# A decoder layer's cross-attention in steps of two head groups, with the feed-forward products of the second sequence's head phase spread in quarters and 32 turns ahead of the first load

## The chip, the cores and the metric

The kernel runs on one core of one Trainium2 chip. The metric is the device time of one execution in microseconds (us); "before" is the median of three runs. Engines are named as in the profile: PE is TensorE (PEld its weight loads, SPq, POOLq and so on an engine's issuing side), DVE is VectorE, ACT is ScalarE, POOL is GpSimd, SP is SyncE, which issues all DMAs.

## The reference, cut to what matters

Two sequences of 1024 tokens with 256 features pass through one post-norm decoder layer: causal self-attention with rotary embedding (16 heads of 16), cross-attention to 77 context tokens, and a feed-forward part of five matrices. Each is followed by a residual addition and a layer norm.

```
x = _layernorm(x + _L0_attn_ref(x, w_qkv, w_proj))
x = _layernorm(x + _L0_xattn_ref(x, ctx_1024, ctx_1024, mask, Wq, bq, Wk, bk, Wv, bv, Wo, bo))
    # q, k, v in 16 heads of 16; scores (1024 x 77 a head), mask, softmax over 77, times v, times Wo
x = _layernorm(x + _L0_ffn_ref(x, w1, w2, h1, h2, w3))
    # silu(x w1) * (x w2), gelu(. h1), gelu(. h2), . w3
```

## The kernel before, in words

Every engine runs its own written-out program, and semaphores are the only ties. There is no scheduler: the order on an engine is the order in which the code issues. `wait(eng, q, name, n)` waits for a counter of sequence q. The stages of a sequence follow one another, and where the first sequence's feed-forward is due, its products are dealt out over the second sequence's stages by a table (`PLAN`, `F_MM`): a slot is one step of a stage, and `f_products(slot, ...)` issues the products of that slot. `f_work` does the other engines' part of a finished group one slot later.

- **Start.** `projections` makes q, k and v token block by token block (8 blocks of 128 tokens): `project_qk` (L557), `project_v` (L566) and, at block 1, `project_ctx` (L575, L578) on TensorE, `rope` (L1097 to L1099) on VectorE, `rope_add` on GpSimd. VectorE and GpSimd first wait for all small weights (`w_in`, nine loads), TensorE for `set_dve` 4 (VectorE's mask work).
- **Self-attention, "S".** Steps -20 to 49. The steps below 0 are the head phase: `turn` (L599) transposes the staged heads, `max_unit` (L613) makes score blocks only to find row maxima, which `reduce_unit` (L1144, L1146) takes on VectorE. A step has up to four units, in pairs on the two halves of the array's rows (partitions 0 to 63 and 64 to 127). In the second sequence they have two PSUM banks, so unit n waits for the reduction of unit n-2. In that phase of the second sequence the first sequence's products (L834, L831, L822) all stand behind the step's units.
- **Cross-attention, "X".** A token block has 4 groups of 4 heads, and a step is one group: 32 steps a sequence. `x_unit` (L740 mask, L743 three products over 64 rows, 312 columns wide) makes the scores in one of two banks, `x_softmax` on VectorE takes the maximum (L1231) and subtracts it (L1235), `x_turn` (L753, four transposes) runs two steps later into one of two banks, `x_exp` (L1011) is ScalarE's, `x_values` (L764) comes four steps later. Once a block, `x_y_evac` (L1019), `x_y_turn` (L775) and `x_y_norm` (L1190, L1192) normalise its output, and the norm chain follows: transpose "yt" (L686, ScalarE L983), "proj" (L694), `residual` with its statistics on VectorE (L1216 or L1219, L1196, L1198), GpSimd's reciprocal root, `ln_finish` (L1203), transpose "xt" (L702, ScalarE L990), then `q_add` (L1224) or `input_lo` (L1241). "yt" and "xt" share bank 0, "proj" and "q" bank 1.

X(0) runs beside nothing but its own norms until its last steps, which take the first w1 and w2 products (slots from `FFN_STEP` to `X_END`). The second sequence's X is the same.

## Time and profile before

| | us |
|---|---|
| median of 3 runs (957.48 to 961.47) | 957.93 |
| the profiled execution's own time | 960.31 |
| its span, first to last instruction | 958.6 |
| TensorE busy | 881.7 (92%) |
| VectorE, ScalarE, GpSimd busy | 507.0, 377.2, 313.2 |

The profile is one execution. Busy time of TensorE is modelled from pipelined instructions that overlap, so 92% does not mean that it works at its peak; what one kind of work costs is read from the distance between the starts of successive instructions. The mean granted clock is 0.956 of full speed.

### The profile page before, as it was taken

To read this page: it belongs to the slowest core of one execution; us is meant where nothing else is said; L and a number is where in the kernel's file an instruction comes from. 1 tells how busy PE (TensorE), PEld (TensorE's weight loads), DVE (VectorE), ACT (ScalarE), POOL (GpSimd) and SP (SyncE) were. 2 spreads that over 40 slices of the span, in tenths; PEclk is the share of its full clock that TensorE was granted. 3 is DMA by queue.
4 is the path that set the end of the run, shared out by engine and by line. 5 is a ranking of instruction groups with operands and counts; after the bars stand their busy time and mean duration, and the time that the engine had idled before them with its cause. 6 is when DMAs were issued, how large, how long until landed. Compare 5 with 4: busy or idle time off the path is not lost.

```text
span 958.6 us, 14238 instructions
## 1 busy us (share of the span) xinstructions
PE 881.7 (92%) x5034; PEld 579.7 (60%) x5034; DVE 507.0 (53%) x1363; ACT 377.2 (39%) x790; POOL 313.2 (33%) x553
## 2 busy tenths in 40 slices
PE   5789999899999999988989899999999999999996
PEld 2544444346666777876666644443476667887885
DVE  4597888526565632165343678883366653116113
ACT  0566666673334311132111166666633343122210
POOL 4403224236101534344222223223440024335332
PEclk9956999989999999999989989998999999999999
DMA  9800533330000322323222033340000000000000
GB/s 310 333 1 3 186 124 133 123 130 1 1 2 1 104 95 92 128 100 121 88 88 88 13 122 133 134 155 2 1 2 1 1 1 1 1 1 23 1 1 24
DMA packets 23896, 68.71 MB, mean 72 GB/s; under 512 B 4400, under 2 KB 11568, under 8 KB 23600
## 3 DMA queue, kind: packets, MB, share of 16 engines
q1 hardware_dynamic: 23824, 67.77, 20.0%
q8 instruction: 43, 0.70, 0.3%
q14 instruction: 29, 0.24, 0.1%
HBM read 65.40 MB, written 13.63 MB: 82 GB/s over the span
## 4 chain that ended last, share of the span: by engine, by line
PE 76%; DVE 13%; issue 4%; ACT 3%; POOL 3%; SPq 1%; DMA 0%; POOLq 0%; DVEq 0%; ACTq 0%
PE bank L834 24%; PE bank L662 7%; PE bank L644 7%; PE bank L613 6%; PE bank L822 4%; PE bank L743 4%; DVE max_raw L1144 4%; PE bank L753 4%; DVE bank L1146 4%; PE bank L831 3%; PE bank L599 3%; PE bank L694 3%; PE bank L557 2%; PE bank L764 2%; PE bank L711 1%
## 5 line engine op out<-in xcount | busy, mean ns | idle before, releaser
L974 ACT ACTIVATE prob_s<-bank 128x512 f32<-128x512 f32 (+3 forms) x384 | 163.5, 497 | 80.3 <-PE bank L644 79.7
L1428 POOL TENSOR_TENSOR hid_lo_s<-act_raw_s,hid_hi_s 128x512 fp32r<-128x512 f32 x96 | 123.7, 1289 | 215.1 <-DVE hid_hi_s L1298 180.3
L613 PE MATMUL bank<-k_t_s,q_t_s 64*128 64x512 f32 (+3 forms) x384 | 141.1, 465 | 26.3 <-DVE max_raw L1146 15.3
L1298 DVE CAST hid_hi_s<-act_raw_s 128x512 fp32r<-128x512 f32 x64 | 30.5, 477 | 195.4 <-ACT act_raw_s L1035 195.1
L1146 DVE CUSTOM_DVE_ANT_0 bank<-bank,causal_bf 128x128 f32<-128x128 f32 (+3 forms) x256 | 122.8, 511 | 18.9 <-PE bank L613 16.8
L1399 POOL TENSOR_SCALAR_AFFINE_SELECT prob_s<-prob_s 128x128 f32<-128x128 f32 x256 | 72.0, 295 | 166.8 <-ACT prob_s L974 163.5
L644 PE MATMUL bank<-q_t_s,k_t_s 64*128 64x512 f32 (+3 forms) x384 | 115.2, 408 | 2.5 <-issue 1.6
L1035 ACT ACTIVATE act_raw_s<-bank,scales 128x512 f32<-128x512 f32 x64 | 43.7, 688 | 183.6 <-PE bank L834 183.6
L613 PEld LDWEIGHTS bank<-k_t_s,q_t_s 64*128 64x128 f32 x384 | 64.9, 205 | 70.2 <-DVE max_raw L1146 30.7
L644 PEld LDWEIGHTS bank<-q_t_s,k_t_s 64*128 64x128 f32 x384 | 58.5, 195 | 76.1 <-ACT prob_s L974 51.9
L1144 DVE TENSOR_REDUCE max_raw<-bank 128x1 f32<-128x512 f32 x128 | 82.4, 685 | 37.2 <-PE bank L613 37.2
L834 PE MATMUL bank<-hid_hi_s,home_s 128*128 128x512 f32 x256 | 99.9, 390 | 0.6 <-POOL hid_lo_s L1428 0.6
L834 PE MATMUL bank<-hid_lo_s,home_s 128*128 128x512 f32 x256 | 99.7, 390 | 0.0
L662 PE MATMUL bank<-prob_s,v_sb_s 128*32 128x512 f32 (+3 forms) x768 | 86.4, 523 | 3.3 <-POOL prob_s L1399 2.8
L834 PE MATMUL bank<-hid_hi_s,ring_s 128*128 128x512 f32 x192 | 78.3, 408 | 0.0
L834 PE MATMUL bank<-hid_lo_s,ring_s 128*128 128x512 f32 x192 | 76.9, 401 | 0.0
L1011 ACT ACTIVATE prob_s<-bank 77x512 f32<-77x512 f32 x64 | 37.9, 592 | 77.7 <-PE bank L753 77.7
L834 PEld LDWEIGHTS bank<-hid_hi_s,home_s 128*128 128x128 f32 x256 | 48.1, 188 | 11.3 <-issue 1.4
L834 PEld LDWEIGHTS bank<-hid_lo_s,home_s 128*128 128x128 f32 x256 | 48.1, 188 | 9.9
L1406 POOL TENSOR_SCALAR ln_var<-ln_mean 128x1 f32<-128x1 f32 x32 | 7.9, 248 | 135.6 <-DVE ln_mean L1198 135.6
L557 PE MATMUL bank<-w_qkv,x_t_s 128*128 128x512 f32 x64 | 32.1, 634 | 12.2 <-DMA w_qkv<-in_w_qkv 9.4
L753 PE MATMUL bank<-ident,xdiff_s 128*77 128x128 f32 x256 | 42.2, 288 | 0.2 <-issue 0.2
(154 smaller groups left out, 1516.1 us busy)
## 6 DMA issues: line engine op xcount, KB each, us to landing
ring_s<-scratch SPq DMA_DIRECT2D x34, 512.0 KB, 3.3
home_s<-scratch SPq DMA_DIRECT2D x22, 512.0 KB, 6.0
checked_s<-in_w_ffn SPq DMA_DIRECT2D x2, 3584.0 KB, 17.8
scratch<-in_w_ffn SPq DMA_DIRECT2D x2, 2560.0 KB, 10.6
ring_moved_s<-scratch SPq DMA_DIRECT2D x10, 512.0 KB, 3.1
checked_s<-in_w_ffn SPq DMA_DIRECT2D x1, 4096.0 KB, 32.2
x_t_s<-in_x_t SPq DMA_DIRECT2D x2, 1024.0 KB, 5.5
x_tok_s<-in_x SPq DMA_DIRECT2D x2, 1024.0 KB, 9.3
```

Of the source, the lines that this page charges most:

```text
L557: i = mm(bank[QK_BANKS[q][t % 2]][:], x_t[q][:, k, P * t:P * (t + 1)], L["w_qkv"][:, k, 0:2 * D], start=k == 0, stop=k == KD - 1)
L613: mm(out[:, 0:k1 - k0], qkt(q, p, 0)[r, P * qt:P * (qt + 1)], qkt(q, p, 1)[r, k0:k1], start=True, stop=True).then_inc(S["max_mm"], 1)
L644: mm(S_BANK[j][:, 0:CHUNK - q0], qkt(q, p, 1)[r, P * kb:P * (kb + 1)], qkt(q, p, 0)[r, CHUNK * c + q0:CHUNK * (c + 1)], start=True, stop=T ...
L662: m = mm(Y[32 * j:32 * (j + 1), q0:CHUNK], v_window(v_sb[q][:, kb], 4 * g + j), prob[q][4 * (s % 2) + j][:, 0:CHUNK - q0], start=kb == 0, ...
L753: m = pe.transpose(out[0:CTX, P * j:P * (j + 1)], xdiff[q][n % 4][:, j, 0:CTX], ident[:])
L834: o = mm(out[:], view(tile_h(f_weights(q, n, 0)[:], k), True), view(src[part][:, k]), start=i == 0, stop=i == last)
L974: act.activation(prob[q][4 * (s % 2) + j][:, 0:n], S_BANK[j][:, 0:n], ACT.Exp, scale=SCALE).then_inc(S["exp_done"], 1)
L1035: act.activation(act_raw[q][r % 3][:], f_bank(n)[:], ACT.Gelu, scale=scales[:, 1 + LAYER_NUMBER[layer], m:m + 1]).then_inc(S["f_act"], 1)
L1144: dve.tensor_reduce(dst, out[:], AXX, ALU.max).then_inc(S["max_red"], 1)
L1146: dve.tensor_tensor_reduce(out=out[:, 0:left], in0=out[:, 0:left], in1=L["causal_bf"][:, CHUNK - left:CHUNK], scale=1.0, scalar=NEG, op0=A ...
L1399: pool.affine_select(out=pr, in_=pr, compare_op=ALU.is_ge, fill=0.0, base=0, pattern=[[1, P]], channel_multiplier=-1).then_inc(S["select_d ...
L1428: pt(dst[1][:, m], act_raw[q][r % 3][:], dst[0][:, m].bitcast(F32), ALU.subtract).then_inc(S["f_lo"], 1)
```

## The change

Four edits. (1) Cross-attention takes two groups a step: 16 steps a sequence. The two groups' units lie in the two banks of one pair (tensor `bank_pair` of two banks), their products alternate between the two halves of the array's rows, and maximum, subtraction and exponential are one instruction each for both groups. There is one pair for units and one for turns, where there were two single banks for each. The turn comes one step later, the values two; on TensorE the values now stand ahead of the turn, and the turn ahead of the products of the slot. ScalarE's "yt" copy and output copy move ahead of the exponential. (2) VectorE's order in a step becomes softmax, finish, residual, output's normalisation; it was softmax, output's normalisation, residual, finish. (3) In self-attention steps a slot's products are issued in four quarters behind the four unit positions. Only the second sequence's head phase has such products. (4) At the start TensorE turns the identity 32 times as soon as GpSimd has written it, ahead of the wait for the first loads; the waits for the small weights move to their first users. The slots of X shrink from 11 to 6 a sequence, so each takes 10 or 11 of the 64 w1 and w2 products instead of 5 or 6.

```diff
+WARM = 32
-XN = NT * NG
-XTURN, XVALUES, XY = 2, 4, 2 * NG + 1
-X_NORM = XY + 2
+XG = NG // 2
+XN = NT * XG
+XTURN, XVALUES, XY = 1, 2, 2 * XG
+X_NORM = XY + 1
 FFN_STEP = XN + 1
-X_END = NG * (NT - 1) + X_NORM + 5
+X_END = XG * (NT - 1) + X_NORM + 4
-    lags = {"yt": (0, 0), "proj": (1, 1), "xt": (3, 4), "q": (4, None)}
+    lags = {"yt": (0, 0), "proj": (1, 1), "xt": (3, 3), "q": (4, None)}
-XUNIT_BANKS = (2, 3)
-XTURN_BANKS = (4, 5)
+XUNIT_PAIR, XTURN_PAIR = 1, 2
...
         def x_unit(q, n):
-            t, g = divmod(n, NG)
+            t, first = n // XG, 2 * (n % XG)
             if n == 0:
                 wait(pe, q, "ctx_blocks", 4)
                 wait(pe, q, "exp_done", 4 * LAST)
-            if g == 0:
+            else:
+                wait(pe, q, "xsub", n)
+            if first == 0:
                 wait(pe, q, "q_hi", t + 1)
                 wait(pe, q, "q_lo", t + 1)
-            if n >= 2:
-                wait(pe, q, "xsub", n - 1)
...
+            for i in range(2):
+                mm(x_units[:, i, 0:4 * CP].rearrange("p (j k) -> p j k", k=CP), L["ident_bf"][:], mask, start=True, stop=False)
+            for part, (of_q, of_k) in enumerate(((0, 0), (0, 1), (1, 0))):
+                for i in range(2):
+                    half, r = (first + i) // 2, slice(SLOT * i, SLOT * (i + 1))
+                    m = mm(x_units[:, i, 0:4 * CP], xq_hl[q][of_q][r, half, P * t:P * (t + 1)],
+                           kx_blocks[of_k][r, half].rearrange("p j k -> p (j k)"), start=False, stop=part == 2)
...
         def x_turn(q, n):
             wait(pe, q, "xsub", n + 1)
-            if n >= 2:
-                wait(pe, q, "xexp_done", n - 1)
+            if n:
+                wait(pe, q, "xexp_done", n)
...
-        def f_products(slot, exact):
+        def f_products(slot, exact, part=0, parts=1):
             if slot is None:
                 return
-            for q, n, i in F_MM[slot]:
+            work = F_MM[slot]
+            for q, n, i in work[len(work) * part // parts:len(work) * (part + 1) // parts]:
                 f_product(q, n, i, exact)
...
                     if kind == "y" and j == 3 and y_step(i) == s:
                         y_turn(q, i)
-            f_products(slot, exact)
+                f_products(slot, exact, j, 4)
...
             if s < XN:
                 x_unit(q, s)
-            if 0 <= s - XTURN < XN:
-                x_turn(q, s - XTURN)
             norm_products(q, "X", s, ("yt", "proj"))
-            f_products(slot, exact)
             if 0 <= s - XVALUES < XN:
                 x_values(q, s - XVALUES)
-            if s >= XY and (s - XY) % NG == 0 and (s - XY) // NG < NT:
-                x_y_turn(q, (s - XY) // NG)
+            if 0 <= s - XTURN < XN:
+                x_turn(q, s - XTURN)
+            if s >= XY and (s - XY) % XG == 0 and (s - XY) // XG < NT:
+                x_y_turn(q, (s - XY) // XG)
+            f_products(slot, exact)
             norm_products(q, "X", s, ("xt", "q"))
...
         pe.wait_ge(set_pool, 11)
-        pe.wait_ge(set_dve, 4)
+        for i in range(WARM):
+            m = pe.transpose(R[:, P * (i % 4):P * (i % 4 + 1)], ident[:], ident[:])
+        m.then_inc(S["warm_mm"], 1)
         wait(pe, 0, "x_t_in", 16)
         pe.wait_ge(L["w_qkv_in"], 16)
         for t in range(NT + V_LAG):
             projections(0, t)
+        pe.wait_ge(set_dve, 4)
...
         def cross_attention(q, s):
             if s < XN:
                 x_softmax(q, s)
-            if s >= XY and (s - XY) % NG == 0 and (s - XY) // NG < NT:
-                x_y_norm(q, (s - XY) // NG)
-            norm_work(q, "X", s)
+            norm_finish(q, "X", s)
+            norm_work(q, "X", s, ("proj",))
+            if s >= XY and (s - XY) % XG == 0 and (s - XY) // XG < NT:
+                x_y_norm(q, (s - XY) // XG)
+            norm_work(q, "X", s, ("rest",))
...
         dve.wait_ge(L["rope_in"], 16 * 2)
-        dve.wait_ge(w_in, 16 * 9)
```

**TensorE in the middle of X(0).** Before, these rows are two groups of a token block, that is two steps. Bank numbers stand behind `bank`, and `xdiff` is the difference that the turn reads, `prob` what the values read.

```order
L740 MATMUL bank3<-xmask_bias,ident_bf 128x312
L743 MATMUL bank3<-kx_blocks_hi,xq_hi_s0_137 128x312
L743 MATMUL bank3<-kx_blocks_lo,xq_hi_s0_137 128x312
L743 MATMUL bank3<-kx_blocks_hi,xq_lo_s0_138 128x312
L753 MATMUL bank5<-ident,xdiff1_s0_142 77x128 x4
L686 MATMUL bank0<-ident,tok0 128x128 x2
L764 MATMUL bank6<-prob3_s0_88,vx 32x128 x4
L702 MATMUL bank0<-ident,tok0 128x128 x2
L740 MATMUL bank2<-xmask_bias,ident_bf 128x312
```

In the changed kernel the same place, one step with both groups, reads so on TensorE:

```order
L745 MATMUL bank_pair1<-xmask_bias,ident_bf 128x312 x2
L749 MATMUL bank_pair1<-kx_blocks_hi,xq_hi_s0_137 128x312 x2
L749 MATMUL bank_pair1<-kx_blocks_lo,xq_hi_s0_137 128x312 x2
L749 MATMUL bank_pair1<-kx_blocks_hi,xq_lo_s0_138 128x312 x2
L691 MATMUL bank_pair0<-ident,tok0 128x128 x2
L772 MATMUL bank_pair3<-xprob3_s0_150,vx 32x128 x8
L760 MATMUL bank_pair2<-ident,xdiff2_s0_143 77x128 x8
L745 MATMUL bank_pair1<-xmask_bias,ident_bf 128x312 x2
```

The masks, the three products, the turns and the values of two groups now stand together, and the values come ahead of the turn. Before, "xt" (L702) followed "yt" (L686) in the same step; now it is gone from this step and stands in the other step of the block, as L707.

**TensorE in the head phase of the second sequence.** Before, one whole step's units and turn (L613, L599) between two slots' products (L834); `k_t0`, `q_t0` are the turned heads of the first pair.

```order
L834 MATMUL bank5<-hid0_lo_s0_161,ring1_s1_177 128x512
L613 MATMUL bank0<-k_t0_s1_74,q_t0_s1_73 128x512
L613 MATMUL bank1<-k_t0_s1_74,q_t0_s1_73 128x512
L599 MATMUL bank6<-ident,stage_q_s1_61 128x128 x4
L613 MATMUL bank0<-k_t0_s1_74,q_t0_s1_73 128x256
L613 MATMUL bank1<-k_t0_s1_74,q_t0_s1_73 128x256
```

After it, two of a step's four units (L618), with the quarter of five products (L842) between them and the turn (L604) behind the second:

```order
L618 MATMUL bank_pair0<-k_t0_s1_74,q_t0_s1_73 128x512
L842 MATMUL bank_pair2<-hid0_lo_s0_167,ring0_s1_182 128x512
L842 MATMUL bank_pair2<-hid0_hi_s0_166,ring0_s1_182 128x512
L842 MATMUL bank_pair2<-hid0_lo_s0_167,ring0_s1_182 128x512
L842 MATMUL bank_pair2<-hid0_hi_s0_166,ring0_s1_182 128x512
L842 MATMUL bank_pair2<-hid0_lo_s0_167,ring0_s1_182 128x512
L618 MATMUL bank_pair0<-k_t0_s1_74,q_t0_s1_73 128x512
L604 MATMUL bank_pair3<-ident,stage_q_s1_61 128x128 x4
L842 MATMUL bank_pair2<-hid0_hi_s0_166,ring1_s1_183 128x512
```

The two units of a pair no longer stand together; each is an island between products.

**VectorE in X(0).** Before, the end of one step with its residual (L1216), and the next step, which ends with the output's normalisation (L1190, L1192):

```order
L1235 TENSOR_TENSOR xdiff0_s0_141<-bank2,xmax 128x4x77
L1216 SCALAR_TENSOR_TENSOR resid0_s0_131<-bank1,no_key,x_tok_s0_57 128x256
L1196 BN_STATS ln_stats<-resid0_s0_131 128x6
L1198 BN_AGGR ln_mean<-ln_stats 128x2
L1231 TENSOR_REDUCE xmax<-bank3 128x4
L1235 TENSOR_TENSOR xdiff1_s0_142<-bank3,xmax 128x4x77
L1190 RECIPROCAL recip<-bank7 128x16
L1192 TENSOR_TENSOR tok0<-bank7,recip 128x256
```

In the changed kernel, one early step with two groups' softmax, finish, residual and normalisation:

```order
L1250 TENSOR_REDUCE xmax<-bank_pair1 128x8
L1254 TENSOR_TENSOR xdiff1_s0_142<-bank_pair1,xmax 128x8x77
L1222 TENSOR_SCALAR tok0<-resid0_s0_131,ln_mean,ln_rstd 128x256
L1238 TENSOR_TENSOR resid1_s0_132<-bank_pair0,x_tok_s0_57 128x256
L1215 BN_STATS ln_stats<-resid1_s0_132 128x6
L1217 BN_AGGR ln_mean<-ln_stats 128x2
L1209 RECIPROCAL recip<-bank_pair3 128x16
L1211 TENSOR_TENSOR tok0<-bank_pair3,recip 128x256
```

The softmax is half as many instructions of twice the width, and residual and normalisation fall into the same step.

## Rows read from the trace of the kernel before

**Rows 1.** The page's chain that ended last, shares of the span by engine.
```profile
PE 76%; DVE 13%; issue 4%; ACT 3%; POOL 3%; SPq 1%; DMA 0%; POOLq 0%; DVEq 0%; ACTq 0%
```

**Rows 2.** Busy us (instructions) by stretch: X(0) to its last softmax, second head phase.
```profile
core 0: us, PE busy (x) PEld busy (x) DVE busy (x) ACT busy (x) POOL busy (x), PEclk, DMA share, GB/s
225.00:303.00 78.00, 75.47 (x612) 50.63 (x611) 50.43 (x122) 28.99 (x60) 16.49 (x31) 1.00 0.01 1
445.00:552.00 107.00, 94.20 (x403) 67.92 (x402) 48.54 (x140) 17.91 (x29) 27.91 (x28) 0.94 0.20 72
```

**Rows 3.** TensorE's waits in 225 to 303 us: total, times, longest.
```profile
PE bank L702 <- ACT y_t_s L983: 2.3, 5, 0.5
```

**Rows 4.** Timeline of TensorE, one group's step of X(0) and the output's turn.
```profile
start us, us, engine line op out<-in xcount [idle before <-releaser]
295.67 0.31 PE L740 MATMUL bank<-xmask_bias,ident_bf 128*128 128x312 bf16 x1
295.91 0.41 PE L743 MATMUL bank<-kx_blocks_hi,xq_hi_s 64*128 64x312 f32 x1
296.16 0.30 PE L743 MATMUL bank<-kx_blocks_lo,xq_hi_s 64*128 64x312 f32 x1
296.30 0.30 PE L743 MATMUL bank<-kx_blocks_hi,xq_lo_s 64*128 64x312 f32 x1
296.53 0.66 PE L753 MATMUL bank<-ident,xdiff_s 128*77 128x128 f32 x4
297.12 0.43 PE L764 MATMUL bank<-prob_s,vx 77*32 77x128 f32 x8
297.48 0.66 PE L775 MATMUL bank<-ident,y_sb_s 128*128 128x128 f32 x4
297.97 0.30 PE L740 MATMUL bank<-xmask_bias,ident_bf 128*128 128x312 bf16 x1
```

**Rows 5.** Timeline of VectorE and ScalarE, durations at two widths each.
```profile
222.50 0.69 DVE L1166 COPY y_sb_s<-bank 128x512 f32<-128x512 f32 x1 [1.41 <-PE bank L662]
...
292.25 0.37 ACT L983 ACTIVATE y_t_s<-bank 128x256 f32<-128x256 f32 x1
...
297.15 0.48 DVE L1235 TENSOR_TENSOR xdiff_s<-bank,xmax 128x308 f32<-128x308 f32 x1
297.23 0.59 ACT L1011 ACTIVATE prob_s<-bank 77x512 f32<-77x512 f32 x1 [2.08 <-PE bank L753]
```

**Rows 6.** TensorE's waits in 445 to 556 us.
```profile
PE bank L613 <- DVE max_raw L1146: 7.4, 5, 1.8
PE bank L613 <- DVE max_raw L1144: 4.6, 16, 0.8
```

**Rows 7.** Timeline of TensorE in one step of the second head phase.
```profile
510.33 0.39 PE L834 MATMUL bank<-hid_hi_s,ring_s 128*128 128x512 f32 x1
510.56 0.39 PE L834 MATMUL bank<-hid_lo_s,ring_s 128*128 128x512 f32 x1
510.87 0.50 PE L613 MATMUL bank<-k_t_s,q_t_s 64*128 64x512 f32 x2
511.30 0.66 PE L599 MATMUL bank<-ident,stage_q_s 128*128 128x128 f32 x4
...
513.69 0.50 PE L834 MATMUL bank<-hid_hi_s,ring_moved_s 128*128 128x512 f32 x1
514.03 0.39 PE L834 MATMUL bank<-hid_lo_s,ring_moved_s 128*128 128x512 f32 x1
```

**Rows 8.** Timeline of the start, and turns at half clock (last row).
```profile
3.78 0.53 POOL L1483 TENSOR_SCALAR_AFFINE_SELECT causal_bf<-causal_bf 128x128 bf16<-128x128 bf16 x1
9.43 5.78 PE L557 MATMUL bank<-w_qkv,x_t_s 128*128 128x512 f32 x8 [9.43 <-DMA w_qkv<-in_w_qkv]
16.17 0.69 DVE L1097 TENSOR_TENSOR rope_a_s<-bank,cos_t 128x512 f32<-128x512 f32 x1 [9.88 <-DMA blocks<-in_blocks]
29.34 1.88 PE L557 MATMUL bank<-w_qkv,x_t_s 128*128 128x512 f32 x4
37.56 1.06 PE L599 MATMUL bank<-ident,stage_q_s 128*128 128x128 f32 x8 [1.16 <-DVE stage_k_s L1132]
61.00 1.09 PE L599 MATMUL bank<-ident,stage_q_s 128*128 128x128 f32 x4 [1.13 <-issue]
```

97 lines of the change are left out of this document (54 added, 43 removed).

## The prediction

> **What bounds the kernel.** I read the chain that ended last first: TensorE holds 76% of it [rows 1]. An edit pays where it makes TensorE's own sequence shorter or takes a wait out of it. The busy time by stretch comes next. In cross-attention up to its last softmax (225 to 303 us, 32 steps) TensorE is busy for 75.5 of 78 us, at full clock, and the other engines for far less [rows 2]; its waits there are 2.3 us, five of about 0.5 us, all "xt" behind ScalarE's "yt" copy out of the bank that both use [rows 3]. So a step takes 78 / 32 = 2.4 us and is TensorE's own work. In the second head phase (445 to 552 us) TensorE is idle for 12.8 of 107 us and its granted clock is 0.94 [rows 2]. Of two levels, 0.94 means 12% of the time at the half one, about 12.8 us in which half the speed is lost: 6.4 us of full-speed work. Its waits there are 12.0 us, all for VectorE's reductions [rows 6].
>
> **Cross-attention: what a pair of groups costs.** "Busy" hides what matters, so I take starts from the timeline of one step [rows 4]. The mask starts at 295.67, the products at 295.91, 296.16 and 296.30, the turns at 296.53: 0.86 us for a unit, of which 0.24, 0.25, 0.14 and 0.23 lie between those starts. 312 columns at 2.4 GHz are 0.13 us, so only the third gap is near its work; the others have 0.1 us on top, where the array goes from one shape of work to another (128 rows, 64 rows, 128 rows) or where the next weights go to the same half. The turns take 0.59 us for four (to 297.12) and the values 0.36 us (to 297.48); the turns themselves run 0.11 us apart, as the output's four show (0.49 us to 297.97).
>
> In the changed step both units stand together, their products alternate between the halves, and each change of shape is paid once for two groups. What two products on different halves cost is in the head phase: two 512-column units in one row end after 0.50 us, and the next work starts 0.43 us after them [rows 7]; two in turn would be 0.21 us longer. So they run beside each other. The pair: masks 0.13 + 0.24, products 0.25 + 0.14 + 0.23, together 0.99 us, against 2 x 0.86 = 1.72: 0.73 saved. Eight turns in a row: 0.59 + 4 x 0.11 = 1.03 against 1.18: 0.15 saved. Sixteen value products: the 0.36 us hold two passes of 0.13, so 0.36 + 0.27 = 0.63 against 0.72: 0.09 saved. That is 0.97 us a pair, **15.5 us a sequence** for 16 pairs. The bound on the other side: if the halves took turns, three products of 0.13 us would come back, 0.39 us a pair or 6.2 us a sequence.
>
> **What it adds there.** With one pair of banks a unit waits for the softmax of the step before. Width costs VectorE (0.69 - 0.48) / 204 = 1.03 ns a column [rows 5], so 616 columns take 0.48 + 0.32 = 0.80 us, twice that for maximum and subtraction. With the last product's 0.30 us [rows 4] and about 0.15 us for three hand-overs the next unit can start 2.05 us after the last product starts. TensorE meanwhile has at least 0.23 + "yt" 0.2 + values 0.63 + turns 1.03 = 2.1 us in the lean step of a block and over 3 us in the other. That is covered, but barely. Not covered is step 1 of each sequence, with only "yt" between the first two units: **1.5 us**. The exponential of 1024 columns takes 0.59 + 2 x 0.22 = 1.0 us [rows 5] and must end ahead of the next values; behind it on ScalarE stands the copy "xt" (0.37 us), then `input_lo`, then "yt" on the same bank. From the end of the turns: 0.2 + 1.0 + 0.4 + 0.5 = 2.1 to 2.2 us, against y turn 0.49 + "xt" 0.25 + unit 0.99 = 1.73 us on TensorE: a new wait of 0.45 us a block for about six blocks, **2.7 us**. At the end, where no unit follows, values and turns wait twice for the exponential, **1.0 us**. The five waits of rows 3 go (2.3 us), since "xt" now stands in the other step. The 64 w1 and w2 products and the rest of the tail are the same work in fewer steps; I count them at nothing. ScalarE's and VectorE's part of them is covered by 10 or 11 products of 0.23 us a slot (2.4 us) against 1.55 us for a pair's activation and gate, and if that cover fails it costs some tenths a slot.
>
> VectorE's new order costs nothing: in a block's fuller step it has 1.6 softmax, 1.1 residual and statistics, 0.7 normalisation and 0.4 `input_lo`, less than TensorE's 4.3 us, and the residual's input is there earlier than the normalisation's.
>
> Sum for a sequence: 15.5 + 2.3 - 1.5 - 2.7 - 1.0 = 12.6 us. Both: **-25.2 us**. Ends: -12.7 (halves take turns) and -32.6 (no new wait but the first).
>
> **Head phase in quarters.** Of 12.0 us of waits [rows 6] nearly all can go: a quarter is 5 products of 0.23 us (510.33 to 510.56 [rows 7]), 1.2 us, longer than a 0.69 us reduction and its hand-over. And with no idle stretches the clock should not fall, which is worth 6.4 us. Against it stand the islands. Going from products into a unit takes 0.31 us instead of 0.23; a unit's way out 0.43 instead of 0.21; and the first product behind it 0.34 instead of 0.23 (513.69 to 514.03) [rows 7]: 0.08 + 0.22 + 0.11 = 0.41 us an island. Before, a step has about 1.0 us of this (one way in and out, and the way to and from the turn); afterwards four islands, 1.7 us. A pair that ran side by side now runs apart, 0.2 us more. That is +0.9 us a step, 13 us in 14 steps. Sum -12.0 - 6.4 + 13 = **-5 us**. Ends: -12 if the islands cost half of that, +3 if the clock falls all the same.
>
> **Start.** Before, the first product starts at 9.43 us, and eight take 5.78 us [rows 8], at full clock 8 x 0.43 = 3.4 (four take 1.88 with their last one's tail). 5.6 us to the eighth's end without its tail are five products at 0.85 and three at 0.43, so the clock rose some 4.3 us after the first one started. The identity is ready at 4.3 us (the last row of GpSimd before it ends at 3.78 + 0.53). A turn is 1.06 / 8 = 0.11 to 0.13 us at full clock, and about 0.22 at the half (four in 1.09) [rows 8]. If turns raise the clock as those products did, it rises at about 8.7 us, after 20 turns; 12 more end at 9.9 to 10.1. The eight products then end at 13.3 instead of 15.0. VectorE's first rotation, which waited until 16.17 for the last small weight, can start at 11.8. TensorE goes on with what lies before the last q/k product at 29.34 [rows 8]: 8.6 us of q/k and 1.7 of v products, and 4.0 us that hold the context's products and waits for VectorE; of these I take 0.6 away, since VectorE's context sums still stand between its rotations. That gives 27.1, **-2.2 us**, which reaches the first turn at 37.56 through rotation, sum and staging unchanged.
>
> The Trainium skill, "TensorE: Matmul & The Clock Gate", Part 4, speaks against this: it says that transposes do not count as TensorE's work for the clock in the way products do. No row here settles that, for no stretch is turns alone. By that rule this term would be the +1.3 us of the third rival below.
>
> **Sum.** -25.2 - 5 - 2.2 = -32.4 us. Against the profiled execution's own 960.31 us that is 927.9. The median of the runs is 2.4 us lower, 957.93, so the time is **925.5 us**.
>
> **Rivals.**
> *Half a gain in cross-attention.* The halves take turns where both accumulate, or VectorE's chain of maximum and subtraction takes 0.4 us longer than its width says and shows in every lean step. X then gives 12 to 16 us, and the time is 935 to 945 us. For it: the margin of the lean step is nil. Against: two units in 0.50 us.
> *The islands eat the head phase.* As many changes of shape again and a clock that still falls: +3 instead of -5, 933 us.
> *Turns do not raise the clock.* 32 turns at half clock end at 4.4 + 7.0 = 11.3 us, the products start 1.9 us late and again at half clock. VectorE's early rotations give back some 0.6 us of this: +1.3 us instead of -2.2, 929 us. I give it 0.4, inside the forecast's own range.
> *No change.* TensorE's sequence gets shorter, but the waits behind it grow as much: 955 to 960 us.
> *Slower.* VectorE is a queue: if in both steps of a block its softmax stands behind `input_lo`, which waits for ScalarE behind the exponential, a step becomes TensorE's whole step plus copy, `input_lo` and the part of the softmax that the unit doesn't cover: 3.6 + 0.4 + 0.4 + 0.9 = 5.3 us against 4.8 for two steps now, +16 us, 974 us. It decides once the new wait is over (25.2 + 5 + 2.2) / 32 = 1.0 us in every step beyond those counted. Only one of a block's two steps has `input_lo`, so I give it little.
>
> **How the numbers follow.** The forecast (X at -20 to -33, head phase at -10 to +1, start at -4 to +1) has 0.62 and 914 to 935 us. Half a gain in X 0.20; the head phase at +3 with a full X 0.05; more than 44 us gained 0.03; no change 0.06; slower 0.04. The range 914 to 941 us takes in the forecast and most of the second and third case. A difference of 0.5% (4.8 us) is about what this measurement can tell from none. Faster by more: 0.62 + 0.20 + 0.05 + 0.03 = 0.90; same 0.06; slower 0.04.
>
> **What would show it.** In the profile after: a pair of units with 0.99 us from mask to the next work and the two products of a pair starting together (1.4 us would be the halves in turns); a token block in 7.2 to 7.7 us instead of 9.6; TensorE's longest wait in X for the subtraction in step 1, 1.5 us, and small ones of "yt" for `input_lo`; maximum and subtraction at 0.80 us each. In the head phase no wait for a reduction over 1 us, a granted clock of 1.00, and 5 us less. At the start, whether the eight q/k products run 0.43 us or 0.85 us apart. The prediction is wrong if TensorE waits in each lean step for the subtraction, or if the islands cost more than 0.41 us.

## The result and the profile after

The changed kernel takes 928.22 us (median of 4 runs, 927.68 to 932.09), beside 959.26 us of the kernel before on the same chip; the ratio is 0.968, with a 95% interval of 0.965 to 0.971. A second set of 6 runs gave 925.39 us and 0.965 (0.961 to 0.970), so the gain is 31 to 33 us. The prediction was 925.5 us, in a range of 914 to 941.

On the page of the changed kernel, the engines' busy time and the chain that ended last, by engine:

```profile
PE 865.7 (93%) x5066; PEld 572.7 (62%) x5066; DVE 499.5 (54%) x1299; ACT 374.1 (40%) x758; POOL 313.4 (34%) x553
PE 78%; DVE 13%; ACT 3%; issue 3%; POOL 2%; POOLq 0%; DVEq 0%; ACTq 0%
```

TensorE held 76% of the chain [rows 1]; it holds 78% of a shorter one. The change shortened TensorE's own sequence and the bound is still there.

I cut each trace into stages at the first instruction of a kind (first staged turn, first unit's score, first mask, first w1 or w2 product, and so on). The table gives each stage's length in us, with the time at half granted clock in parentheses. The zeros of the first row mean little: the trace holds no clock record for its first 9 to 14 us, in which TensorE ran at half speed. "Again" is the changed kernel's second profile; "best" is the last kernel of this study.

```
stage                          before       after        again        best
start, to the first turn       37.6 ( 0)    35.0 ( 0)    35.2 ( 0)    35.1 ( 0)
first head phase               40.8 (34)    40.7 (29)    40.8 (33)    40.7 (29)
self-attention 0              147.1 (17)   146.2 (15)   146.2 (15)   146.0 (15)
cross-attention 0              80.5 ( 0)    67.3 ( 0)    67.4 ( 0)    64.7 ( 0)
w1 and w2 slots behind it      22.0 ( 0)    20.4 ( 0)    20.3 ( 0)    20.3 ( 0)
q/k/v products 1               94.0 ( 3)    95.0 ( 3)    95.0 ( 3)    95.2 ( 7)
second head phase             129.2 (14)   122.3 ( 0)   122.3 ( 0)   106.1 ( 0)
self-attention 1              146.2 (14)   153.9 (41)   146.3 (14)   146.0 (14)
cross-attention 1              80.3 ( 0)    67.2 ( 0)    67.2 ( 0)    64.7 ( 0)
w1 and w2 slots behind it      20.7 ( 0)    19.2 ( 0)    19.2 ( 0)    19.2 ( 0)
feed-forward to the end       160.2 ( 3)   163.1 ( 7)   161.5 ( 4)   161.5 ( 3)
```

The change's three places give 2.4 us (start), 14.7 us a sequence (cross-attention and the slots behind it) and 6.9 us (head phase). The two cross-attention rows have to be read together. In the kernel before, the values of three groups (1.1 us) and one turn of the output (0.4 us) lie behind the first w1 or w2 product; in the changed kernel they lie ahead of it. So 1.5 of the 1.6 us that the second row lost only moved to the first. The one stage of before against after that goes the other way is self-attention 1, where no instruction changed: in that execution its clock was at the half level for 41 us. In "again" it wasn't, and the span was 921.4 us instead of 930.3.

*Cross-attention.* Busy time by stretch in the profile after, to be held against rows 2 (the first line is the block of X(0), the second the head phase):

```profile
219.00:285.00 66.00, 62.60 (x640) 47.12 (x642) 47.33 (x97) 28.39 (x47) 17.29 (x32) 1.00 0.01 1
420.00:530.00 110.00, 108.06 (x435) 69.48 (x434) 55.44 (x156) 22.12 (x35) 32.23 (x35) 0.99 0.23 75
```

The timeline of TensorE in one token block of the first cross-attention, after:

```profile
257.61 0.43 PE L745 MATMUL bank_pair<-xmask_bias,ident_bf 128*128 128x312 bf16 x2
...
259.05 0.41 PE L691 MATMUL bank_pair<-ident,tok 128*128 128x128 f32 x2 [0.38 <-DVE x_lo_s L1260]
259.39 0.65 PE L772 MATMUL bank_pair<-xprob_s,vx 77*32 77x128 f32 x16
259.96 1.10 PE L760 MATMUL bank_pair<-ident,xdiff_s 128*77 128x128 f32 x8
260.90 0.44 PE L745 MATMUL bank_pair<-xmask_bias,ident_bf 128*128 128x312 bf16 x2
261.27 0.41 PE L749 MATMUL bank_pair<-kx_blocks_hi,xq_hi_s 64*128 64x312 f32 x2
261.52 0.30 PE L749 MATMUL bank_pair<-kx_blocks_lo,xq_hi_s 64*128 64x312 f32 x2
261.66 0.31 PE L749 MATMUL bank_pair<-kx_blocks_hi,xq_lo_s 64*128 64x312 f32 x2
261.89 1.13 PE L699 MATMUL bank_pair<-w_o,y_t_s 128*128 128x256 f32 x4
262.95 0.65 PE L772 MATMUL bank_pair<-xprob_s,vx 77*32 77x128 f32 x16
263.53 1.10 PE L760 MATMUL bank_pair<-ident,xdiff_s 128*77 128x128 f32 x8
264.46 0.60 PE L783 MATMUL bank_pair<-ident,y_sb_s 128*128 128x128 f32 x4
264.90 0.38 PE L707 MATMUL bank_pair<-ident,tok 128*128 128x128 f32 x2
265.12 0.44 PE L745 MATMUL bank_pair<-xmask_bias,ident_bf 128*128 128x312 bf16 x2
```

A pair of units takes 0.99 us (260.90 to 261.89), where two single ones took 1.72 [rows 4]: the gaps are 0.37, 0.25, 0.14 and 0.23, the ones that the prediction added up. The two products of one row cost the gap of one, so the halves work side by side. The values take 0.57, the turns 0.93. The block is 7.51 us (257.61 to 265.12), inside the 7.2 to 7.7 forecast.

TensorE's waits in this cross-attention, after (total, times, longest), and VectorE's two wide operations:

```profile
PE bank_pair L691 <- DVE x_lo_s L1260: 2.8, 5, 1.3
PE bank_pair L745 <- DVE xdiff_s L1254: 1.5, 1, 1.5
PE bank_pair L772 <- ACT xprob_s L1023: 0.2, 1, 0.2
...
250.74 0.80 DVE L1250 TENSOR_REDUCE xmax<-bank_pair 128x8 f32<-128x616 f32 x1 [0.47 <-PE bank_pair L749]
251.58 0.80 DVE L1254 TENSOR_TENSOR xdiff_s<-bank_pair,xmax 128x616 f32<-128x616 f32 x1
```

The forecast said 2.7 us for "yt" behind `input_lo`, 1.5 us in step 1, 0.80 us at 616 columns, and no wait in the lean steps. All four stand here. The end of the sequence waits 0.2 us and not 1.0.

*Head phase.* Its reductions held TensorE for 13.3 us before; rows 6 show 12.0 of them, because their window opens 23 us after the phase begins. None of these waits is left from 404 to 530 us after. The first two lines are before (421.9 to 551.2 us), the third is the longest that is left, after, on the first score behind the phase:

```profile
PE bank L613 <- DVE max_raw L1146: 8.7, 6, 1.8
PE bank L613 <- DVE max_raw L1144: 4.6, 16, 0.8
...
PE bank_pair L649 <- DVE resid_f_s L1285: 1.7, 1, 1.7
```

*Start.* TensorE from its first instruction on, after: the first 22 turns, the last 11 (the windows share one), the first eight products, and VectorE's first rotation; the last row is the busy time of 4.1 to 8.8 us, with the columns of rows 2:

```profile
4.13 4.95 PE L919 MATMUL bank_pair<-ident 128*128 128x128 f32 x22 [4.13 <-POOL causal_bf L1511]
8.66 1.51 PE L919 MATMUL bank_pair<-ident 128*128 128x128 f32 x11
10.01 3.60 PE L562 MATMUL bank_pair<-w_qkv,x_t_s 128*128 128x512 f32 x8
12.03 0.69 DVE L1116 TENSOR_TENSOR rope_a_s<-bank_pair,cos_t 128x512 f32<-128x512 f32 x1 [4.12 <-PE bank_pair L562]
...
4.10:8.80 4.70, 4.67 (x22) 4.67 (x23) 3.75 (x3) 0.00 (x0) 2.44 (x3) 1.00 1.04 389
```

From 4.13 to 8.66 us the turns start (8.66 - 4.13) / 21 = 0.22 us apart, from there to 10.01 1.35 / 11 = 0.12 us. The level went from the half to the full one near 8.7 us, with only turns on TensorE so far, and the eight products ran at 0.43 us each. The prediction had 8.7, 9.9 to 10.1, and 11.8 for the rotation.

### The profile page after: what moved, and what is told of

Same layout as the page of the kernel before. It is cut to its first block, busy times and chain, and to the rows that moved or that the text cites. A ratio compares the mean times of both kernels' runs of the same rounds, so it can differ in the third digit from the quotient of the medians.

```text
span 930.3 us, 14113 instructions
## 1 busy us (share of the span) xinstructions
PE 865.7 (93%) x5066; PEld 572.7 (62%) x5066; DVE 499.5 (54%) x1299; ACT 374.1 (40%) x758; POOL 313.4 (34%) x553
## 4 chain that ended last, share of the span: by engine, by line
PE 78%; DVE 13%; ACT 3%; issue 3%; POOL 2%; POOLq 0%; DVEq 0%; ACTq 0%
PE bank_pair L842 25%; PE bank_pair L667 7%; PE bank_pair L649 7%; PE bank_pair L618 7%; PE bank_pair L830 6%; DVE bank_pair L1165 4%; PE bank_pair L760 4%; DVE max_raw L1163 3%; PE bank_pair L699 3%; PE bank_pair L839 3%; PE bank_pair L604 3%; PE bank_pair L562 2%; PE bank_pair L772 2%; PE bank_pair L749 2%; PE bank_pair L716 1%
## 5 line engine op out<-in xcount | busy, mean ns | idle before, releaser
L986 ACT ACTIVATE prob_s<-bank_pair 128x512 f32<-128x512 f32 (+3 forms) x384 | 163.5, 495 | 86.7 <-PE bank_pair L649 85.8
L618 PE MATMUL bank_pair<-k_t_s,q_t_s 64*128 64x512 f32 (+3 forms) x384 | 149.2, 467 | 13.7 <-DVE max_raw L1165 7.6
L1165 DVE CUSTOM_DVE_ANT_0 bank_pair<-bank_pair,causal_bf 128x128 f32<-128x128 f32 (+3 forms) x256 | 123.4, 509 | 54.0 <-PE bank_pair L618 52.6
L649 PE MATMUL bank_pair<-q_t_s,k_t_s 64*128 64x512 f32 (+3 forms) x384 | 119.0, 423 | 3.9 <-DVE resid_f_s L1285 1.7
L618 PEld LDWEIGHTS bank_pair<-k_t_s,q_t_s 64*128 64x128 f32 x384 | 68.7, 207 | 62.9 <-issue 20.3
L1163 DVE TENSOR_REDUCE max_raw<-bank_pair 128x1 f32<-128x512 f32 x128 | 83.0, 685 | 43.1 <-PE bank_pair L618 43.1
L842 PE MATMUL bank_pair<-hid_hi_s,home_s 128*128 128x512 f32 x256 | 100.9, 394 | 1.7 <-POOL hid_lo_s L1455 1.7
L842 PE MATMUL bank_pair<-hid_lo_s,home_s 128*128 128x512 f32 x256 | 100.6, 393 | 0.0
L667 PE MATMUL bank_pair<-prob_s,v_sb_s 128*32 128x512 f32 (+3 forms) x768 | 89.6, 541 | 3.2 <-POOL prob_s L1426 2.7
L842 PE MATMUL bank_pair<-hid_hi_s,ring_s 128*128 128x512 f32 x192 | 79.2, 413 | 0.0
L842 PE MATMUL bank_pair<-hid_lo_s,ring_s 128*128 128x512 f32 x192 | 77.7, 405 | 0.0
L842 PEld LDWEIGHTS bank_pair<-hid_hi_s,home_s 128*128 128x128 f32 x256 | 48.6, 190 | 13.0 <-issue 2.9
L842 PEld LDWEIGHTS bank_pair<-hid_lo_s,home_s 128*128 128x128 f32 x256 | 48.6, 190 | 10.1
L842 PEld LDWEIGHTS bank_pair<-hid_lo_s,ring_s 128*128 128x128 f32 x192 | 36.1, 188 | 11.0 <-issue 4.2
L842 PEld LDWEIGHTS bank_pair<-hid_hi_s,ring_s 128*128 128x128 f32 x192 | 36.1, 188 | 10.2 <-issue 2.8
```

Source lines behind the costliest of these rows:

```text
L618: mm(out[:, 0:k1 - k0], qkt(q, p, 0)[r, P * qt:P * (qt + 1)], qkt(q, p, 1)[r, k0:k1], start=True, stop=True).then_inc(S["max_mm"], 1)
L649: mm(S_BANK[j][:, 0:CHUNK - q0], qkt(q, p, 1)[r, P * kb:P * (kb + 1)], qkt(q, p, 0)[r, CHUNK * c + q0:CHUNK * (c + 1)], start=True, stop=T ...
L667: m = mm(Y[32 * j:32 * (j + 1), q0:CHUNK], v_window(v_sb[q][:, kb], 4 * g + j), prob[q][4 * (s % 2) + j][:, 0:CHUNK - q0], start=kb == 0, ...
L842: o = mm(out[:], view(tile_h(f_weights(q, n, 0)[:], k), True), view(src[part][:, k]), start=i == 0, stop=i == last)
L986: act.activation(prob[q][4 * (s % 2) + j][:, 0:n], S_BANK[j][:, 0:n], ACT.Exp, scale=SCALE).then_inc(S["exp_done"], 1)
L1163: dve.tensor_reduce(dst, out[:], AXX, ALU.max).then_inc(S["max_red"], 1)
```

## The experiments

All ratios are to the kernel before on the same chip, with a 95% interval. Stage lengths are those of the table's stages.

**The changed kernel once more (again).** No edit.

> The changed kernel once more, as the base for its relatives. In its first profile the second sequence's self-attention (first score to first cross-attention unit) took 153.9 us against 146.2 us before, with the clock at half for 34 us there against 14 us before, though no instruction of that stage moved. Theory: an execution's own luck with the clock, then this profile shows the stage at 146 to 149 us and an own time near 928 us. Rival: the change brings it about (the stage begins in another phase), then it is again over 152 us. Time 926 to 930 us either way, 31 us under before.

Measured: 925.39 us, 0.965 (0.961 to 0.970), span 921.4 us. Of the 8.9 us to the first profile's span, most are self-attention 1 (7.6 us, 41 against 14 us at half clock; the expectation had the 41 as 34) and the end (1.6 us). The expectation stands: the stage's length was that execution's and not the change's. The yardstick for the runs below is this profile.

**The start without the turns (no_turns).**

```
-        for i in range(WARM):
-            m = pe.transpose(R[:, P * (i % 4):P * (i % 4 + 1)], ident[:], ident[:])
-        m.then_inc(S["warm_mm"], 1)
```

> The 32 turns at the start left out, the moved waits kept. Theory (turns raise the clock): the first q/k products run 0.85 us apart until about 4.3 us after the first one, which starts at 9.4 us; the first turn of the staged heads comes at 36.5 to 37.5 us instead of 35.0, so 1.5 to 2.5 us slower than the changed kernel. Rival (what helped is only that VectorE no longer waits for the small weights): first staged turn at 35.0 to 35.5 us and the same time.

TensorE's first products in this kernel, the first five and the last four of eight (one is in both):

```profile
9.26 3.97 PE L562 MATMUL bank_pair<-w_qkv,x_t_s 128*128 128x512 f32 x5 [9.26 <-DMA w_qkv<-in_w_qkv]
12.64 1.88 PE L562 MATMUL bank_pair<-w_qkv,x_t_s 128*128 128x512 f32 x4
12.94 0.69 DVE L1113 TENSOR_TENSOR rope_a_s<-bank_pair,cos_t 128x512 f32<-128x512 f32 x1 [5.02 <-PE bank_pair L562]
```

The first four products are 0.85 us apart ((12.64 - 9.26) / 4), like the first five before. The rotation starts at 12.94, already 3.2 us earlier than before [rows 8], because VectorE no longer waits there for the last small weight. The first staged turn is at 35.9 us: 0.7 us later than with the turns (35.2), 1.7 us earlier than before (37.6), and between the theory's 36.5 and the rival's 35.5. Whole: 929.60 us, 0.968 (0.964 to 0.973); the interval overlaps that of "again", so the stage carries the verdict.

The stage varies too: in the ten profiles of this study that have the turns, the first staged turn lies between 34.5 and 35.8 us (mean 35.2). Its distance from the first product does not vary: 25.0 us in all ten, 26.7 us here, 28.0 to 28.3 us in the three profiles with the old start. What varies is when the clock rises and with it when the 32 turns end, and the first product waits for that: it starts at 9.45 to 10.8 us, where without turns it starts at 9.26. So the turns save 1.7 us and give about 0.9 of it back by ending after the weights have come. The moved waits gave some two thirds of the start's gain and the turns some one third; on the side without turns this is one profile. Fewer turns might keep more; no run has tried.

**The head's products all behind the units again (no_quarters).**

```
-                f_products(slot, exact, j, 4)
+            f_products(slot, exact)
```

> The slot's products in one piece behind the four units again, all else as changed. Theory: in the second head phase the waits for reductions return (12 us) and with them the half clock, while the islands go: 5 to 7 us slower than the changed kernel. Rival (the gain of that phase came from elsewhere, as its other start): within 2 us.

Measured: 934.02 us, 0.973 (0.969 to 0.977); second head phase 126.4 us (7 at half clock) against 122.3, 4.1 us where 5 to 7 were expected. The median differs by 8.6 us; in this profile the rest lies in stages that the edit does not touch (self-attention 1 took 150.4 us with 27 at half clock). Its waits:

```profile
PE bank_pair L618 <- DVE max_raw L1165: 8.7, 6, 1.8
PE bank_pair L618 <- DVE max_raw L1163: 4.6, 16, 0.8
```

This stage runs the same code here and in the kernel before, with 7 and 14 us at half clock: (129.2 - 126.4) / 7 = 0.4 us for each. At full clock it would take 123.6 us, and without its 13.3 us of waits 110.3. With quarters it takes 122.3, so breaking the units up costs 12.0 us more than it did here, by this estimate. It is not the price of all islands, for the waits broke pairs up too: the second pair of a step stood behind the reductions of the first. Of the phase's 30 pairs 15 start together in this kernel and in the one before, none with quarters, and 27 with the halves of a later run.

**One group's three products, then the other's (one_half).** The loops over `part` and `i` in `x_unit` change places.

```
-            for part, (of_q, of_k) in enumerate(((0, 0), (0, 1), (1, 0))):
-                for i in range(2):
+            for i in range(2):
+                for part, (of_q, of_k) in enumerate(((0, 0), (0, 1), (1, 0))):
```

> A unit pair's six products in the order of the groups (three on one half of the rows, then three on the other) instead of alternating. Theory (alternating products of a pair run side by side, others do not): 0.25 + 2 x 0.14 us come back for each of 32 pairs, cross-attention 0.4 to 0.55 us a step longer, 13 to 17 us slower than the changed kernel in all. Rival (what was saved is the number of changes of shape alone, and the halves take turns in any order): under 0.1 us a step, within 3 us.

Measured: 927.42 us, 0.965 (0.961 to 0.969), cross-attention 67.3 us as in "again". The expectation fell. The timeline of one pair in this kernel:

```profile
261.38 0.44 PE L745 MATMUL bank_pair<-xmask_bias,ident_bf 128*128 128x312 bf16 x2
261.74 0.42 PE L749 MATMUL bank_pair<-kx_blocks_hi,xq_hi_s 64*128 64x312 f32 x2
...
262.37 1.13 PE L699 MATMUL bank_pair<-w_o,y_t_s 128*128 128x256 f32 x4
```

The pair takes 0.99 us in this order too, and the products of the two groups still start together (0.01 us apart) although one group's three are written first. Whether the hardware or the build of the program brought them together, the trace does not tell. The alternation in the code buys nothing; the next run tests what does.

**The two units of a pair one behind the other (apart).** Each group's mask stands directly ahead of its own products; one softmax, one set of turns and values for the pair as in the changed kernel.

```
             for i in range(2):
                 mm(x_units[:, i, 0:4 * CP]..., L["ident_bf"][:], mask, start=True, stop=False)
-            for part, ... in enumerate(((0, 0), (0, 1), (1, 0))):
-                for i in range(2):
+                for part, ... in enumerate(((0, 0), (0, 1), (1, 0))):
```

> In a pair the second group's mask stands behind the first group's three products instead of with the first mask, so the array changes from 128-row to 64-row work and back once more a pair; all else as changed. Theory (standing together is what saves, by fewer changes of shape and by running both halves at once): a pair takes 1.7 us from its mask to the next work instead of 0.99, cross-attention up to its last turn grows by 0.7 x 16 = 11 us a sequence, 20 to 23 us in all, time 946 to 949 us. Rival (the saving came from longer instructions on VectorE and ScalarE and from fewer steps): the pair is longer but waits shrink as much, within 5 us of the changed kernel.

Measured: 953.28 us, 0.992 (0.989 to 0.995). One pair in this kernel:

```profile
265.61 0.30 PE L745 MATMUL bank_pair<-xmask_bias,ident_bf 128*128 128x312 bf16 x1
265.84 0.41 PE L748 MATMUL bank_pair<-kx_blocks_hi,xq_hi_s 64*128 64x312 f32 x1
...
266.46 0.31 PE L745 MATMUL bank_pair<-xmask_bias,ident_bf 128*128 128x312 bf16 x1
...
267.33 1.13 PE L699 MATMUL bank_pair<-w_o,y_t_s 128*128 128x256 f32 x4
```

1.72 us a pair instead of 0.99, to the hundredth what two single units took before. Cross-attention is 80.3 us against 67.4, 12.9 more, where 11 were expected. The parts: 16 pairs by 0.73 = 11.7; the waits of "yt" fall from 2.8 to 1.3 us; and 7 us at half clock cost 3.5 if half the speed is lost there, as the second cross-attention of the run yt_late below bears out. That is 13.7, 0.8 more than measured. What counts is thus that no product on all rows stands between the two groups. With the slots behind it, the grouping leaves (80.5 + 22.0) - (80.3 + 20.4 - 3.5) = 5.3 us a sequence without it, as much as turns and values save in longer rows (the last part has them).

**VectorE's old order (dve_old).** The finish of the norm moves back behind the residual as well.

```
+            if s >= XY and (s - XY) % XG == 0 and (s - XY) // XG < NT:
+                x_y_norm(q, (s - XY) // XG)
+            norm_work(q, "X", s, ("proj",))
             norm_finish(q, "X", s)
-            norm_work(q, "X", s, ("proj",))
-            if s >= XY and (s - XY) % XG == 0 and (s - XY) // XG < NT:
-                x_y_norm(q, (s - XY) // XG)
```

> VectorE's old order in cross-attention steps (normalisation, residual, finish), all else as changed. Theory of the prediction (the order costs and gives nothing, VectorE has room in the fuller step): within 2 us. Rival: the normalisation waits for the output's turn at the end of TensorE's step, so the residual (1.1 us) moves behind it and the next softmax with it; TensorE then waits in the lean step for the subtraction or for the low part, 0.7 to 1.0 us a block, 9 to 14 us in all.

Measured: 941.56 us, 0.980 (0.976 to 0.983), the rival's case and more; cross-attention 73.8 us against 67.4. The slots behind it took 21.9 us against 20.3, but with 3.4 us at half clock and the same waits (1.0 and 0.9 us): their first eleven products took 4.2 us instead of 2.7, which is the whole difference. The second sequence shows the same. TensorE's waits in the first cross-attention, and VectorE in one block of it:

```profile
PE bank_pair L691 <- DVE x_lo_s L1260: 6.7, 5, 2.1
...
PE bank_pair L716 <- DVE resid_s L1235: 1.1, 1, 1.1
PE bank_pair L716 <- DVE resid_s L1238: 1.0, 1, 1.0
...
258.47 0.80 DVE L1254 TENSOR_TENSOR xdiff_s<-bank_pair,xmax 128x616 f32<-128x616 f32 x1
260.73 0.26 DVE L1209 RECIPROCAL recip<-bank_pair 128x16 f32<-128x16 f32 x1 [1.46 <-PE bank_pair L783]
...
261.37 0.47 DVE L1235 SCALAR_TENSOR_TENSOR resid_s<-bank_pair,no_key,x_tok_s 128x256 f32<-128x256 f32 x1
```

VectorE is idle for 1.46 us, waiting for the output's turn, with the residual queued behind that wait although its input is ready. The residual, its statistics and `input_lo` then come late in the next step, and TensorE waits for them: 6.7 + 1.1 + 1.0 us of waits against 2.8, 6.0 of the 6.4 us.

**"yt" behind the values (yt_late).** Found from the waits of the profile after.

```
-            norm_products(q, "X", s, ("yt", "proj"))
+            norm_products(q, "X", s, ("proj",))
             if 0 <= s - XVALUES < XN:
                 x_values(q, s - XVALUES)
+            norm_products(q, "X", s, ("yt",))
```

> The transpose yt stands behind the values instead of ahead of them, all else as changed. Theory (TensorE's 2.8 us of waits a sequence are yt waiting for VectorE's low part, which comes 0.4 us later): the values cover it, 2.5 us less a sequence, 4 to 5 us in all, 921 us. Rival: the wait moves to the next unit, which waits for the subtraction, since VectorE's chain is what bounds the lean step: under 1 us.

Measured: 922.35 us, 0.959 (0.955 to 0.964). The first cross-attention is 64.7 us instead of 67.4, and no wait for `x_lo` is left. The 2.7 us are the 2.8 us of waits that the prediction priced at 2.7. In the second, which had 3.4 us at half clock in this profile, it is 66.3, against 64.7 for the same code at full clock in the last run below: half the speed was lost there.

**The head's products in halves (halves).**

```
-                f_products(slot, exact, j, 4)
+                if j % 2:
+                    f_products(slot, exact, j // 2, 2)
```

> The slot's products in two halves, behind the second and the fourth unit, so that the units of a pair stand together again; all else as changed. Theory (an island costs 0.41 us and a pair apart 0.2 us, and 2.4 us of products cover two reductions of 0.7): the second head phase takes 116 to 119 us instead of 122.3, 3 to 6 us faster. Rival: what counts is that a reduction never has two units before it, waits of 0.3 us for the second reduction return in each step, within 1 us of the quarters.

Measured: 911.06 us, 0.947 (0.944 to 0.951), head phase 106.1 us. The gain is 16.2 us, three times what I expected. TensorE in a step of the changed kernel with quarters (of its second profile):

```profile
442.10 0.39 PE L842 MATMUL bank_pair<-hid_lo_s,ring_s 128*128 128x512 f32 x1
442.42 0.49 PE L618 MATMUL bank_pair<-k_t_s,q_t_s 64*128 64x512 f32 x1
442.84 0.50 PE L842 MATMUL bank_pair<-hid_hi_s,ring_moved_s 128*128 128x512 f32 x1
443.18 0.40 PE L842 MATMUL bank_pair<-hid_lo_s,ring_moved_s 128*128 128x512 f32 x1
```

and with halves:

```profile
442.31 0.39 PE L842 MATMUL bank_pair<-hid_lo_s,ring_s 128*128 128x512 f32 x1
442.62 0.49 PE L618 MATMUL bank_pair<-k_t_s,q_t_s 64*128 64x512 f32 x2
443.05 0.66 PE L604 MATMUL bank_pair<-ident,stage_q_s 128*128 128x128 f32 x4
```

A unit alone takes the same 0.42 to 0.43 us as two units on different rows (442.42 to 442.84, 442.62 to 443.05). In quarters each unit stands alone between products on all rows, so the second one of a pair, which is free beside the first, costs a whole island: 0.32 us into it, 0.42 out, 0.34 to the second product, less two products of 0.23, is 0.62 us at 512 columns. The units are entered from other work 60 times in this phase with quarters and 30 times with halves; 16.2 / 30 = 0.54 us, a mean over the narrower units too. By the distances from start to start, the 60 units take 11.8 us with halves, 21.8 with quarters and 17.7 in the kernel before, where half of the pairs stood apart. Halves still hide the reductions: TensorE is busy for 105.6 of 106 us here:

```profile
404.00:510.00 106.00, 105.61 (x513) 78.83 (x513) 58.75 (x164) 26.90 (x41) 39.35 (x38) 1.00 0.32 106
```

**Three islands a step (three).**

```
-                f_products(slot, exact, j, 4)
+                if j == 1:
+                    f_products(slot, exact, 0, 2)
+                if j > 1:
+                    f_products(slot, exact, j, 4)
```

> The changed kernel, with the head's products in three portions a step: half of them behind the first two units, a quarter behind the third unit and a quarter behind the fourth. So the first pair of units of a step runs side by side and the second pair apart: three islands of units a step, where quarters have four and halves two. The head phase took 122.3 us with four islands a step and 106.1 with two. Theory: what quarters lose against halves is a fixed price for each island that a single unit makes (0.33 us into it and 0.37 us out of it in place of 0.23 us for one product, 0.46 us an island, and the second unit of a pair for nothing when they stand together), so three islands lie in the middle: head phase 114 us, span 8 us below the changed kernel's, median about 918. Rival: the loss comes from something that quarters as a whole do (products that wait for their weights or banks when they come in small portions); then the step with any quarter in it pays nearly all of it and the head phase stays at 119 us or above.

Measured: 915.72 us, 0.954 (0.950 to 0.958), head phase 115.1 us. Four, three and two islands give 122.3, 115.1 and 106.1 us: 7.2 and 9.0 us for one more a step (60, 45 and 30 entries into units; TensorE waits 0.9 us in this run and 0.4 with halves), so the loss goes with their number and not with quarters as such. The rival's 119 us is excluded.

**Parts of the change in the kernel before (b_quarters, b_halves).** The kernel before with this edit alone; the second one has `if j % 2: f_products(slot, exact, j // 2, 2)` there.

```
+                f_products(slot, exact, j, 4)
-            f_products(slot, exact)
```

> The kernel before with one part of the change alone: the head's products in quarters. Theory: the parts add up, and this one is worth in the kernel before what the stage lengths say, head phase 129 us to 122 us, of which the larger part is the half clock that goes with the waits for the reductions. Median 7 us below the kernel before, ratio 0.993. Rival: in the kernel without quarters but with the rest of the change the head phase took 126.4 us, so quarters are worth 4 us and the ratio is 0.996; by the prediction's own terms (waits 12.0, clock 6.4, islands 13) it is 5 us.

> The kernel before with the head's products in halves and nothing else of the change. Theory: two islands a step with the pairs side by side hide the reductions as four do and pay for half the islands, so the head phase goes from 129 us to 106 us, 23 us: more than twice what quarters give, and nearly as much as the whole change of cross-attention. Median about 937, ratio 0.976. Rival: the gain of halves needs something else of the change; then the head phase lands above 115 us.

Measured: quarters 957.74 us, 0.996 (0.993 to 0.998), head phase 122.4 us; halves 939.69 us, 0.977 (0.972 to 0.982), head phase 105.9. Both stages land where they do in the changed kernel, so this part is independent of the rest. Quarters' 6.8 us in the stage show as about 4 us in the median; self-attention 0 had 30 us at half clock in both profiles and took 151 us instead of 147, which may hide the rest; that is not shown.

**Halves and "yt" behind the values (yt_halves), "best" in the table.** The edits of halves and yt_late together.

> The changed kernel with both improvements that the runs so far point to: the head's products in halves, and in cross-attention the turn called yt issued behind the values and not ahead of them, so that it no longer waits for VectorE's input_lo. Theory: the two lie in different stages and add up. Halves took 16.2 us off the head phase; yt behind the values took 2.7 us off the first sequence's cross-attention (67.4 to 64.7) and should take as much off the second where the clock does not fall. Together about 21 us below the changed kernel: median 905, range 902 to 909. Rival: with the wait gone the clock falls in the second cross-attention as it did in the run with yt behind the values alone (66.3 us with 3 us at half clock); then only 17 us, median 909.

Measured: 902.02 us (900.19 to 906.40), 0.940 (0.936 to 0.944), at the lower end of the forecast's 902 to 909. Both cross-attentions take 64.7 us and the head phase 106.1. By the ratios it is 2.6 to 2.9% faster than the changed kernel (0.940 / 0.965, 0.940 / 0.968).

## Why the prediction was right, and where it was not

*Cross-attention, -12.6 us forecast, -14.7 measured a sequence, with the slots that the forecast counted in at nothing.* The steps hold. Added up over both stages of the first sequence by the distances from start to start, waits left out, units went from 27.4 to 16.1 us (11.3 saved, 11.7 forecast), turns from 17.6 to 14.9 (2.7, 2.4 forecast) and values from 11.9 to 9.2 (2.7, 1.4 forecast): 16.6 against the forecast's 15.5. Step 1 cost the 1.5 us, "yt" 2.8 (2.7 by taking it away) for 2.7, and the end 0.2 for 1.0. The 2.3 us of rows 3 are gone. So the mis-sized terms are the values (1.3 us more saved) and the end (0.8 us less lost); with the turns' 0.3 more and the units' 0.4 less they bring 12.6 to 14.6. "I count them at nothing" holds: in the slots two waits of 0.7 and 0.5 us went and one of 1.0 us came. The rival "half a gain" has a slip of its own: 12 to 16 us in cross-attention give 935 to 939 us by its terms, and 945 only if another part fails too.

*"VectorE's new order costs nothing"* was true and missed the point: it is worth 6.4 us a sequence in cross-attention. In the old order the change would have brought 8.3 of its 14.7. I added up VectorE's work a block (3.8 us) and compared it with TensorE's 4.3; the row shows that its length was not the matter, but the residual's place behind a wait of 1.46 us for the output's turn. The forecast was right only because its sum assumed that no such wait arises, and the new order is what keeps that so. This would have been the rival "half a gain in cross-attention", by a mechanism that I did not name. Whether the half clock in the slots of that run comes from the waits ahead of it is not shown.

*Head phase, -5 forecast, -6.9 measured.* Waits -13.3, not the 12.0 of the forecast's window; clock, 14 us by the measured 0.4, 5.6 against 6.4; that leaves 12.0 us for the islands, as in the run without quarters, against 13. The size was right as a sum, and partly by luck: the terms in it were not. The forecast took the pairs before as side by side, though half of them stood apart behind their waits. And "a pair that ran side by side now runs apart, 0.2 us more" was too small: a single unit costs as much as a pair (0.42 us against 0.43), so the partner's island costs 0.5 us and more. What I never asked is whether two islands would hide the reductions as well; they do, and that was worth more (16.2 us) than the whole head-phase edit. In the expectation of that run I priced it from the same 0.2 us and was wrong by a factor of three.

*Start, -2.2 forecast, -2.4 and -2.5 measured.* The times inside it stood (clock up at 8.7, products at 10.0, rotation 12.03 against 11.8). The attribution did not: I gave nearly all of the gain to the turns, and some 1.7 us of it come from the moved waits. The rival "turns do not raise the clock" is excluded: the spacing of the turns falls from 0.22 to 0.12 us with no other work on TensorE, and without turns TensorE is still at half speed until 12.6 us, so it is not the time since the start that does it. The rule of the Trainium skill ("TensorE: Matmul & The Clock Gate", Part 4), that transposes don't count for the clock as products do, is not borne out by this trace of float32 turns; the measurement decides. By that rule the start would have come out at +1.3 us; it is at -2.4.

*What stays open.* The parts sum to -38.7 us (2.4 + 2 x 14.7 + 6.9) and the spans of before and "again" differ by 37.2. Of the end's 1.3 us more, 1.1 is one more wait for GpSimd just behind the last transpose, here in the end of "again" and of the kernel before:

```profile
PE bank_pair L842 <- POOL hid_lo_s L1455: 1.7, 2, 0.9
...
PE bank L834 <- POOL hid_lo_s L1428: 0.6, 1, 0.6
```

It is in every profile with the new cross-attention, and what brings it about is not shown. The second q/k/v stage's 1.0 us need not be of the change: without any half clock the stage took 93.5 us both in yt_late and in b_quarters. The medians differ by only 31 to 33, because the clock in unchanged stages differs from one execution to the next.

## What to carry to other kernels

Count the places where TensorE goes from work on all rows to work on half of them and back, not only the products: a lone half-row product cost as much as two on different halves, so keep partners together and split filler work only as finely as the waits need. When a wait sits in an in-order queue, look at what is queued behind it and already has its input; moving the residual ahead of one 1.5 us wait was worth 6.4 us a sequence, over two fifths of cross-attention's gain. When an edit has two parts at one place (turns and moved waits), run the one without the other before giving either the credit.

## What the runs showed of the hardware

- The order in which products on different row halves are written did not matter within a group of six: written group by group, they still ran side by side (0.99 us a pair either way).
- Turns of 128 by 128 in float32 alone took TensorE from the half level (1.2 GHz) to the full one (2.4): at 8.7 us in this profile, and at 7.6 to 10.3 us in the other nine that have the turns. The granted clock reads 1.00 for all of the stretch before (the last row of the start's fence), because the trace has no clock record there yet; only the spacing shows the level.
- Self-attention, with the same instructions, took between 145.7 and 153.9 us over the profiles of this study, with 14 to 41 us at half clock. The stage grows by about 0.3 us for each us at half clock ((153.9 - 146.2) / (41 - 14)), the head phase with its waits by 0.4, and cross-attention, which TensorE nearly fills, by 0.5 ((66.3 - 64.7) / 3.4). A single profile can therefore hide a gain of 8 us; the stage lengths, with the half-clock time beside them, could be read to 0.1 us.
